# A decoder layer on one core: first loads spread over the turns, a table of context parts for each block, and three parts behind the last tile

## The chip, the core and the metric

The kernel runs on one core of one Trainium2 chip. TensorE (PE), VectorE (DVE), ScalarE (ACT), GpSimd (POOL) and SyncE (SP) run their own instruction streams and meet at semaphores. The metric is the device time in microseconds (us), from the first to the last instruction and what the launch lays around it; less is better.

## The reference, cut to what matters

One layer of a decoder: self-attention, cross-attention to a context, and a feed-forward part, each followed by a layer norm. The first half of the kernel, which the change touches, computes this:

```python
# x [8, 512, 512]: t = 8 positions, 512 columns of the batch, 512 features; 16 heads of 32
qkv = x @ in_proj_weight.T + in_proj_bias
p = (pos @ pos_proj_weight.T + pos_proj_bias).reshape(-1, h, d)
ac = jnp.einsum('tbhd,sbhd->bhts', q + r_w_bias, k)
bd = jnp.einsum('tbhd,rhd->bhtr', q + r_r_bias, p)      # then a relative shift
attn = jax.nn.softmax((ac + bd) * scale, axis=-1)
ctx = jnp.einsum('bhts,sbhd->tbhd', attn, v).reshape(t, b, e)
x = _layernorm(x + ctx @ out_proj_weight.T + out_proj_bias)
# for the second half: keys and values of the context (ctx_2048 [8, 512, 1024])
src_trans = (jnp.einsum('bsf,of->bso', src, W_src) + b_src) * src_mask[:, :, None]
```

The second half (cross-attention of 8 heads, feed-forward with rounding to an 8-bit format) reads the first half's output, the keys and the values from scratch tensors in HBM.

## The kernel before, in words

**Blocks and steps.** The first half (`phase_a`) cuts the 512 columns into NB = 4 blocks of 128 partitions. A block has 16 steps: eight score steps, in which VectorE multiplies one position's query with all keys (`score_products`) and sums over a head (`score_sums`); then the softmax; and eight value steps (`context_products`, `context_sums`), each giving one tile `ctx1` of the attention's result. Four more steps, 64 to 67, clear what is left. In the value steps TensorE makes the projections q, k and p of the next block, in the score steps v of this one. Two steps after a tile's value step comes its output projection (`output_projection`, bank `om_b`); VectorE adds the residual and takes the moments, GpSimd and ScalarE normalise, and `store_x1` stores it.

**Context parts.** Beside this run 64 parts of the context's keys and values (`QUARTERS`, the program calls them quarters too). Four parts, n%4 = 0 to 3, make a group: they read the same transposed context `cT`, made of four row blocks. Part n%4 = 0 or 1 has 50 matmuls of 256 columns, part 2 or 3 has 25 of 512. The class `FirstHalf` says how many parts a step has, in one list over the steps. In the step of part n the context rows of number n+5 are converted as well, so the last row block of a group comes with part 2 of the group before (row block 23, say, with part 18) and the group's first part can't start before it is turned.

**How a row block gets to TensorE.** SP loads it; ScalarE rounds it to float16 (`row_hi`, into one of three buffers `rows16`, which must be turned before they are used again), GpSimd makes the rest (`row_lo`), SP issues two DMA transposes (`turn`, into xT, cT or c1T). All of SP's DMAs, loads, turns and stores, go through its one in-order stream, as do those that ScalarE issues through its own. A context row is turned one step after it is converted; `exponentials` stands on ScalarE behind the row conversions of its step.

**Banks.** A part writes one of three banks `sm_b` and waits until VectorE has made `stage_lo` of part n-3; VectorE makes it one step after the part, behind that step's first product.

**The opening.** SP loads row block 0 of x, the key weights (4 x 256 KB), then x 1 to 7, and turns them as they are converted. ScalarE's queue loads the query weights (`wq_n`, 1 MB), later the position weights (`wp_n`) and the value weights (`wv_n`). TensorE transposes the weights, four transposes to a job, and alternates them with the projections k of tiles 0 to 7.

## Time and profile before

| | |
|---|---|
| median of 3 runs | 1966.91 us (1964.98 to 1968.69) |
| profiled execution | 1969.68 us, its span 1967.9 us |
| granted TensorE clock, mean | 0.981 of full speed |
| PE busy | 1849.9 us (94%) |
| DVE busy | 1336.4 us (68%) |
| ACT busy | 785.5 us (40%) |
| POOL busy | 507.2 us (26%) |
| HBM | 94.75 MB read, 33.55 MB written |

The first half ends near 847 us, when the barrier between the halves opens; the blocks' first score products start at 57.08, 252.03, 444.25 and 633.02 us. The shares above are means over both halves. TensorE's busy time counts pipelined matmuls and says nothing of how fast they run; the two levels of its clock are 1.2 and 2.4 GHz, a granted clock of 0.5 or 1.0.

### The profile page before, as it was taken

To read this page: it belongs to the slowest core of one execution; us is meant where nothing else is said; L and a number is where in the kernel's file an instruction comes from. 1 tells how busy PE (TensorE), PEld (TensorE's weight loads), DVE (VectorE), ACT (ScalarE), POOL (GpSimd) and SP (SyncE) were. 2 spreads that over 40 slices of the span, in tenths; PEclk is the share of its full clock that TensorE was granted. 3 is DMA by queue.
4 is the path that set the end of the run, shared out by engine and by line. 5 is a ranking of instruction groups with operands and counts; after the bars stand their busy time and mean duration, and the time that the engine had idled before them with its cause. 6 is when DMAs were issued, how large, how long until landed. Compare 5 with 4: busy or idle time off the path is not lost. (4 is left out here: it accounts for less than half of the span.)

```text
span 1967.9 us, 33393 instructions
## 1 busy us (share of the span) xinstructions
PE 1849.9 (94%) x12588; PEld 1016.7 (52%) x12588; DVE 1336.4 (68%) x1704; ACT 785.5 (40%) x1208; POOL 507.2 (26%) x548
## 2 busy tenths in 40 slices
PE   6998999898999999977999999999999999999988
PEld 3665455544654566545555455454454554544543
DVE  2897998799889989857565555655655556556521
ACT  3422222222222222238465364462653644626522
POOL 2134964386259326600000100001001000010010
PEclk9999999999999999979999999999999999999999
DMA  8435347525643457566312304204123041041000
GB/s 208 119 80 133 94 113 157 117 75 139 158 97 84 116 146 160 153 134 199 64 51 43 94 21 103 54 1 105 52 42 95 21 103 54 1 103 33 12 33 22
DMA packets 292139, 176.60 MB, mean 90 GB/s; under 512 B 195071, under 2 KB 248319, under 8 KB 291998
## 3 DMA queue, kind: packets, MB, share of 16 engines
q1 hardware_dynamic: 285984, 171.03, 35.6%
q10 hardware_dynamic: 6014, 3.49, 0.8%
q8 instruction: 114, 1.87, 0.4%
q14 instruction: 27, 0.22, 0.0%
HBM read 94.75 MB, written 33.55 MB: 65 GB/s over the span
## 5 line engine op out<-in xcount | busy, mean ns | idle before, releaser
L1468 DVE TENSOR_TENSOR p_lo<-k,p_hi 128x1024 f16<-128x1024 f32 x128 | 156.8, 1225 | 194.1 <-ACT p_hi L1356 194.1
L82 POOL TENSOR_TENSOR vsb<-mvb,consts 128x1 f32<-128x1 f32 x64 | 12.1, 190 | 1029.9 <-DVE mvb L1483 1029.9
L1157 PE MATMUL b_ff<-x2T_hi,w1T_hi 128*128 128x512 f16 x512 | 195.3, 381 | 2.3 <-DVE x2T_lo L1468 2.3
L1513 DVE CUSTOM_DVE_ANT_0 junk<-b_sx,mneg 128x512 f16<-128x512 f32 x256 | 176.1, 688 | 30.3 <-issue 22.3
L1157 PE MATMUL b_ff<-x2T_lo,w1T_hi 128*128 128x512 f16 x512 | 195.3, 381 | 0.0
L1157 PE MATMUL b_ff<-x2T_hi,w1T_lo 128*128 128x512 f16 x512 | 195.1, 381 | 0.0
L1388 ACT ACTIVATE k<-b_st,mbias 128x512 f32<-128x512 f32 x256 | 161.8, 685 | 14.0 <-PE b_st L1201 13.9
L574 PE MATMUL sm_b<-cT_hi,wsT_hi 128*128 128x256 f16 x512 | 142.7, 279 | 24.0 <-DMA cT_lo<-rows_lo 18.6
L775 DVE TENSOR_TENSOR prod<-q,k 128x4096 f32<-128x4096 f32 x32 | 143.1, 4472 | 20.1 <-ACT q L652 19.2
L1356 ACT ACTIVATE p_hi<-k 128x1024 f16<-128x1024 f32 x128 | 135.3, 1057 | 44.1 <-PE b_av L1216 41.7
L540 PE MATMUL pj_b<-winT_hi,xT_hi 128*128 128x512 f16 x384 | 147.3, 384 | 5.2 <-DMA xT_lo<-rows_lo 5.2
L1380 ACT ACTIVATE hq<-b_ff,b 128x512 fp8e4<-128x512 f32 x128 | 88.0, 687 | 156.6 <-PE b_ff L1157 149.9
L540 PE MATMUL pj_b<-winT_lo,xT_hi 128*128 128x512 f16 x384 | 147.2, 383 | 0.0
L540 PE MATMUL pj_b<-winT_hi,xT_lo 128*128 128x512 f16 x384 | 147.1, 383 | 0.0
L815 DVE TENSOR_TENSOR prod<-pr,v 128x4096 f32<-128x4096 f32 x32 | 142.4, 4451 | 1.1
L574 PE MATMUL sm_b<-cT_lo,wsT_hi 128*128 128x256 f16 x512 | 142.8, 279 | 0.0
L574 PE MATMUL sm_b<-cT_hi,wsT_lo 128*128 128x256 f16 x512 | 142.6, 279 | 0.0
L780 DVE TENSOR_REDUCE pr<-prod 128x128 f32<-128x4096 f32 x32 | 141.1, 4410 | 0.1
L437 POOL TENSOR_TENSOR rows_lo<-cn,rows_hi 128x512 f16<-128x512 f32 x64 | 98.5, 1546 | 79.0 <-ACT rows_hi L636 78.9
L1365 ACT ACTIVATE q<-q,rstdb 128x512 f32<-128x512 f32 x64 | 52.1, 814 | 161.7 <-POOL rstdb L88 161.7
L1157 PE MATMUL b_ff<-w2T,hq 128*128 128x512 fp8e4 x512 | 112.9, 379 | 1.6 <-ACT hq L1380 1.0
L1213 PEld LDWEIGHTS b_av<-v_hi,p_hi 128*128 128x128 f16 x1024 | 92.6, 98 | 32.1 <-DVE p_lo L1468 30.9
(270 smaller groups left out, 4318.1 us busy)
## 6 DMA issues: line engine op xcount, KB each, us to landing
cn<-in_ctx_dram SPq DMA_DIRECT2D x64, 256.0 KB, 3.3
k<-kT_scratch SPq DMA_DIRECT2D x24, 512.0 KB, 8.0
x<-in_x_dram SPq DMA_DIRECT2D x32, 256.0 KB, 3.0
x_scratch<-x SPq DMA_DIRECT2D x32, 256.0 KB, 2.2
q<-x_scratch SPq DMA_DIRECT2D x8, 1024.0 KB, 5.6
q<-x_scratch SPq DMA_DIRECT2D x32, 256.0 KB, 4.0
out_dram<-q SPq DMA_DIRECT2D x32, 256.0 KB, 3.8
xn<-in_x_dram SPq DMA_DIRECT2D x24, 256.0 KB, 2.9
```

The lines of the kernel that those rows point to most:

```text
L437: pool.tensor_tensor(lo[:, :], row_source(kind, i), hi[:, :], ALU.subtract).then_inc(s["row_lo"], 1)
L540: pe.matmul(out, a, c, start=(j == 0 and m == 0), stop=False)
L574: pe.matmul(dst, a, z, start=(j == 0 and m == 0), stop=False)
L775: dve.tensor_tensor(prod[:, :, :], q[:, t, :].unsqueeze(1).to_broadcast([P, T, E]), k[:, :, :], ALU.mult).then_inc(s["sc_prod"], 1)
L780: dve.tensor_reduce(pr[:, t].rearrange("p h s -> p s h"), prod[:, :, :].rearrange("p s (h d) -> p s h d", h=H1), AX.X, ALU.add).then_inc(s ...
L815: dve.tensor_tensor(by_head(prod), probs, by_head(v), ALU.mult).then_inc(s["av_prod"], 1)
L1157: mm = pe.matmul(out, a, c, start=(start and n == 0), stop=end)
L1213: pe.matmul(dst, hi[:, st, rows], v_hi[:, st, h, :], start=(st == 0), stop=False)
L1356: act.activation(dst, src, ACT.Copy, scale=scale).then_inc(done, 1)
L1388: act.activation(pf[:, st, :], st_b[st % 2][:, :], ACT.Exp, bias=mbias[:, st:st + 1], scale=D2 ** -0.5).then_inc(s["st_exp"], 1)
L1468: dve.tensor_tensor(dst, bank, hi, ALU.subtract).then_inc(out, 1)
L1513: dve.tensor_tensor_reduce(junk[:, :], sx_b[tt % 2][:, :], mneg[:, :], 1.0, NEG, ALU.add, ALU.max, mx[:, h % 2, tt:tt + 1]).then_inc(s["sx ...
```

## The change

It does four things. (1) SP loads x 3 to 7 one at a time, each behind the turn of the row block three before it; the loads `load_ring` and the first context rows move behind turns 5 to 7. On ScalarE's queue the query weights go behind the conversion of the key weights, in four DMAs instead of one, the position weights two projections later and the value weights three later. (2) The row of positions has a semaphore of its own, so its transposes don't wait for the three columns of biases. (3) The counts of context parts differ by block. In the table below a stroke joins parts of one step; it is worked out from the two lists:

```
            score steps (8)                         value steps (8)
block 1  b  8/9 10 11 12/13 14 15 16/17 18          19/20 21 22 - - - - -
         a  8/9 10 11 12/13 14 15 16/17 18          19 20/21 22 - - - - -
block 2  b  23/24 25 26 27/28 29 30 31/32 33        34/35 36 37 - - - - -
         a  23 24/25 26 27 28/29 30 31 32/33        34 35 36/37 - - - - -
block 3  b  38/39 40 41 42/43 44 45 46/47 48        49/50 51/52 53/54 55/56 57/58 59/60 61/62 63
         a  38 39 40/41 42 43 44/45 46 47           48/49 50/51 52/53 54/55 56/57 58 59 60
after    b  -
         a  61/62 63
```

(4) In steps 64 and 65 TensorE makes the parts 61, 62 and 63, each step's parts ahead of its output projection.

```diff
-    SCORES_FIRST = (0, 0, 0, 0, 1, 1, 1, 1)
-    SCORES = (2, 1, 1, 2, 1, 1, 2, 1)
-    VALUES = (2, 1, 1, 0, 0, 0, 0, 0)
-    VALUES_LAST = (2, 2, 2, 2, 2, 2, 2, 1)
+    SCORES = ((0, 0, 0, 0, 1, 1, 1, 1), (2, 1, 1, 2, 1, 1, 2, 1), (1, 2, 1, 1, 2, 1, 1, 2), (1, 1, 2, 1, 1, 2, 1, 1))
+    VALUES = ((2, 1, 1, 0, 0, 0, 0, 0), (1, 2, 1, 0, 0, 0, 0, 0), (1, 1, 2, 0, 0, 0, 0, 0), (2, 2, 2, 2, 2, 1, 1, 1))
+    TAIL = (2, 1, 0, 0)
...
-            for t in range(1, T):
-                sp.dma_start(k[:, t, :], x_in[0, t]).then_inc(x_first[t], 16)
+            for t in range(1, 3):
+                load_first_x(t)
             for kind, i in plan.first_uses:
                 if kind == "x" or i < 4:
                     turn(kind, i)
+                if kind == "x" and i + 3 < T:
+                    load_first_x(i + 3)
                 if (kind, i) == ("x", 1):
                     load_mask(0)
-                if kind == "x" and 2 <= i < 5:
-                    load_ring(i - 2)
+                if kind == "x" and 5 <= i:
+                    load_ring(i - 5)
...
-                pe.wait_ge(s["small_ld"], 16 * 4)
+                pe.wait_ge(s["pos_ld"], 16)
...
             for g in range(8, plan.STEPS):
+                tail = g >= 16 * NB
+                if tail:
+                    for n in plan.quarters(g):
+                        context_products(n)
                 for n in plan.tiles(g - 2):
                     output_projection(n)
-                for n in plan.quarters(g):
-                    context_products(n)
+                if not tail:
+                    for n in plan.quarters(g):
+                        context_products(n)
...
-            act.dma_start(wq_n, d.in_w[0:E, :].rearrange("(o p) k -> p o k", p=P)).then_inc(win_ld["wq"], 16)
             for n in range(WK, WQ):
                 weights_hi(n)
                 if n % 2:
                     row_hi(*firsts[(n + 1) // 2])
+            for o in range(4):
+                act.dma_start(wq_n[:, o, :], d.in_w[o * P:(o + 1) * P, :]).then_inc(win_ld["wq"], 16)
...
-                if t == 0:
+                if t == 2:
                     for o in range(4):
                         act.dma_start(wp_n[o], d.pos_w[o * P:(o + 1) * P, :]).then_inc(win_ld["wp"], 16)
-                if t == 2:
+                if t == 5:
                     act.dma_start(wv_n, d.in_w[2 * E:3 * E, :].rearrange("(o p) k -> p o k", p=P)).then_inc(
```

SP's stream at its start, before (`k` is the buffer of x, `prod` that of the key weights, `rows_0` to `rows_2` the converted rows):

```order
L374 DMA k<-in_x_dram 128x512
L376 DMA prod<-in_in_w_dram 128x512 x4
L378 DMA k<-in_x_dram 128x512 x7
L330 DMA_TRANSPOSE xT_hi<-rows_0_hi 128x4x128 [waits A_row_lo]
L330 DMA_TRANSPOSE xT_lo<-rows_0_lo 128x4x128
L330 DMA_TRANSPOSE xT_hi<-rows_1_hi 128x4x128 [waits A_row_lo]
L330 DMA_TRANSPOSE xT_lo<-rows_1_lo 128x4x128
```

and of the change:

```order
L373 DMA k<-in_x_dram 128x512
L377 DMA prod<-in_in_w_dram 128x512 x4
L373 DMA k<-in_x_dram 128x512 x2
L328 DMA_TRANSPOSE xT_hi<-rows_0_hi 128x4x128 [waits A_row_lo]
L328 DMA_TRANSPOSE xT_lo<-rows_0_lo 128x4x128
L373 DMA k<-in_x_dram 128x512
L328 DMA_TRANSPOSE xT_hi<-rows_1_hi 128x4x128 [waits A_row_lo]
L328 DMA_TRANSPOSE xT_lo<-rows_1_lo 128x4x128
```

Five of the seven loads have left the place ahead of the first turn. ScalarE's stream at the start of block 1's value steps, before (`pr<-pr` is the exponential):

```order
L636 ACTIVATE rows_1_hi<-xn 128x512 [waits A_xn_ld1,A_turned1]
L636 ACTIVATE rows_2_hi<-cn 128x512 [waits A_cn_ld0,A_turned2]
L636 ACTIVATE rows_0_hi<-cn 128x512 [waits A_cn_ld1,A_turned0]
L672 ACTIVATE pr<-pr 128x1024 [waits A_probs]
L662 ACTIVATE stage_hi<-sm_b,small 128x512 [waits A_mk_scaled,A_st_out1,A_sm_filled]
L662 ACTIVATE stage_hi<-sm_b 128x512 [waits A_st_out0,A_sm_filled]
```

and of the change:

```order
L644 ACTIVATE rows_1_hi<-xn 128x512 [waits A_xn_ld1,A_turned1]
L644 ACTIVATE rows_2_hi<-cn 128x512 [waits A_cn_ld0,A_turned2]
L680 ACTIVATE pr<-pr 128x1024 [waits A_probs]
L670 ACTIVATE stage_hi<-sm_b,small 128x512 [waits A_mk_scaled,A_st_out1,A_sm_filled]
L660 ACTIVATE q<-pj_b 128x512 [waits A_pj_filled,A_sc_done]
```

One context row and its wait for a turned buffer no longer stand ahead of the exponential; in blocks 0 and 3 that row stays. VectorE's end of the first half, before, from the last tile's last sum (`ctx<-prod`) on:

```order
L826 TENSOR_TENSOR ctx<-prod 128x512 [waits A_av_half,A_row_lo]
L764 SCALAR_TENSOR_TENSOR stage_lo<-sm_b,small,stage_hi 128x512 [waits A_sm_hi]
L832 SCALAR_TENSOR_TENSOR x_0<-om_b,x_0 128x512 [waits A_res_ld0,A_om_filled]
L835 BN_STATS small<-x_0 128x6 [waits A_om_used]
L837 BN_AGGR small<-small 128x2 [waits A_ln_stats]
L832 SCALAR_TENSOR_TENSOR x_1<-om_b,x_1 128x512 [waits A_res_ld1,A_om_filled]
```

and of the change:

```order
L835 TENSOR_TENSOR ctx<-prod 128x512 [waits A_av_half,A_row_lo]
L773 SCALAR_TENSOR_TENSOR stage_lo<-sm_b,stage_hi 128x512 [waits A_sm_hi]
L841 SCALAR_TENSOR_TENSOR x_0<-om_b,x_0 128x512 [waits A_res_ld0,A_om_filled]
L844 BN_STATS small<-x_0 128x6 [waits A_om_used]
L846 BN_AGGR small<-small 128x2 [waits A_ln_stats]
L773 SCALAR_TENSOR_TENSOR stage_lo<-sm_b,stage_hi 128x512 [waits A_sm_hi]
L773 SCALAR_TENSOR_TENSOR stage_lo<-sm_b,small,stage_hi 128x512 [waits A_sm_hi]
L841 SCALAR_TENSOR_TENSOR x_1<-om_b,x_1 128x512 [waits A_res_ld1,A_om_filled]
```

Four `stage_lo` instead of one come after the last tile: three of them behind it here, and one more, of part 63, after the last rows shown.

## Rows read from the trace of the kernel before

**Rows 1.** Windows: length; busy PE, PEld, DVE, ACT, POOL; granted clock; DMA share; GB/s
```profile
444.00:633.00 189.00, 180.18 (x1097) 104.36 (x1096) 169.06 (x94) 50.41 (x87) 110.95 (x67) 0.98 0.49 119
633.00:847.00 214.00, 198.06 (x1181) 117.69 (x1179) 184.45 (x110) 47.44 (x76) 103.28 (x77) 0.96 0.56 140
```

**Rows 2.** Waits of TensorE, 0 to 57 us: total, times, longest
```profile
PE om_b L487 <- DMA bcols<-in_rr_dram: 5.5, 1, 5.5
PE pj_b L540 <- DMA xT_lo<-rows_lo: 5.2, 2, 3.0
```

**Rows 3.** Source and tile views, opening: wq load, first transposes, wp loads
```profile
L723 ACTq DMA_DIRECT2D v<-in_in_w_dram x1: 742/742/742, 5.7 to 5.7; - x1
...
DMA to landing us min/median/max: 14.7/14.7/14.7
...
L330 SPq DMA_TRANSPOSE xT_hi<-rows_hi x8: 1200/1319/3103, 7.6 to 41.5; - x8
...
DMA to landing us min/median/max: 2.6/5.3/12.5
...
L737 ACTq DMA_DIRECT2D cT_hi<-in_pos_w_dram x2: 352/401/450, 26.8 to 27.2; - x2
...
DMA to landing us min/median/max: 2.9/3.5/4.1
```

**Rows 4.** Timeline, opening: start, duration, engine, what, [idle before <- releaser]
```profile
11.51 1.39 DVE L842 SCALAR_TENSOR_TENSOR winT_lo<-sm_b,winT_hi 128x512 f16<-128x512 f32 x2 [0.31 <-ACT winT_hi L677]
...
20.67 0.59 PE L540 MATMUL pj_b<-winT_hi,xT_hi 128*128 128x512 f16 x1 [3.00 <-DMA xT_lo<-rows_lo]
...
25.74 0.61 PE L543 MATMUL pj_b<-rows,pick 128*128 128x512 f16 x1
...
29.22 0.38 PE L543 MATMUL pj_b<-rows,pick 128*128 128x512 f16 x1
...
32.46 0.38 PE L543 MATMUL pj_b<-rows,pick 128*128 128x512 f16 x1
```

**Rows 5.** Timeline of block 1, around its exponential and a later residual
```profile
354.13 0.63 ACT L636 ACTIVATE rows_hi<-cn 128x512 f16<-128x512 f32 x1 [2.07 <-DMA cT_lo<-rows_lo]
...
354.25 0.37 PE L574 MATMUL sm_b<-cT_hi,wsT_hi 128*128 128x256 f16 x1 [5.67 <-DMA cT_lo<-rows_lo]
...
355.74 1.22 DVE L801 TENSOR_REDUCE ctx<-pr 128x128 f32<-128x1024 f32 x1 [8.58 <-ACT pr L672]
...
397.35 0.69 DVE L832 SCALAR_TENSOR_TENSOR x<-om_b,x 128x512 f32<-128x512 f32 x1 [2.55 <-PE om_b L555]
```

**Rows 6.** Waits of block 2, 444 to 633 us
```profile
PE sm_b L574 <- DMA cT_lo<-rows_lo: 6.5, 1, 6.5
DVE ctx L801 <- ACT pr L672: 5.6, 1, 5.6
...
DVE x L832 <- PE om_b L555: 2.8, 1, 2.8
```

**Rows 7.** Waits of block 3, 633 to 847 us
```profile
DVE x L832 <- PE om_b L555: 13.0, 6, 8.1
...
PE om_b L554 <- DMA c1T_lo<-rows_lo: 4.2, 1, 4.2
...
PE sm_b L574 <- DVE stage_lo L764: 3.9, 1, 3.9
...
PE sm_b L574 <- DMA cT_lo<-rows_lo: 3.2, 2, 2.9
```

**Rows 8.** Timeline, last matmul of output projections (L555) and of a part
```profile
823.98 0.38 PE L555 MATMUL om_b<-rows,pick 128*128 128x512 f16 x1
...
829.38 0.38 PE L583 MATMUL sm_b<-rows,pick 128*128 128x512 f16 x1
...
832.18 0.38 PE L555 MATMUL om_b<-rows,pick 128*128 128x512 f16 x1
...
841.88 0.44 PE L555 MATMUL om_b<-rows,pick 128*128 128x512 f16 x1
```

More of the change, by code:

```diff
@@ L136, in __init__ @@
         for b in range(NB):
-            counts += self.SCORES if b else self.SCORES_FIRST
-            counts += self.VALUES if b < NB - 1 else self.VALUES_LAST
+            counts += self.SCORES[b] + self.VALUES[b]
+        counts += self.TAIL
         at, self.by_step = 0, []
@@ L154, in quarters @@
     def quarters(self, g):
-        return self.by_step[g] if 0 <= g < 16 * NB else []
+        return self.by_step[g] if 0 <= g < self.STEPS else []
     def tiles(self, g):
@@ L239, in phase_a @@
     pos_b, gb = om_b[1], om_b
-    names = ("made", "zeroed", "step", "small_ld", "bias_ld", "wt_filled", "wt_hi", "wt_lo", "pos_filled", "pos_ready",
+    names = ("made", "zeroed", "step", "small_ld", "pos_ld", "bias_ld", "wt_filled", "wt_hi", "wt_lo", "pos_filled", "pos_ready",
              "pb_ready", "g0_filled", "g_filled", "g_hi", "g_lo", "row_hi", "row_lo", "pj_filled", "pj_copied", "sm_filled", "sm_hi", "sm_lo", "om_filled", "om_used",
@@ L388, in _ @@
                 if kind == "c" and i + 2 < 5:
-                    load_rows(kind, i + 2)
+                    load_rows("c", i + 2)
             for use in plan.loads_after(-1):
@@ L470, in weight_transposes @@
                     if n % 4 == 0:
-                        pe.wait_ge(win_ld[("wk", "wq", "wp", "wv")[n // 4]], 64 if n in (WK, WP) else 16)
+                        pe.wait_ge(win_ld[("wk", "wq", "wp", "wv")[n // 4]], 16 if n == WV else 64)
                 else:
@@ L867, in bias_columns @@
             def bias_columns():
-                dve.wait_ge(s["small_ld"], 16 * 4)
+                dve.wait_ge(s["small_ld"], 16 * 3)
                 for z in range(2):
```

6 lines of the change are left out of this document (4 added, 2 removed).

## The prediction, made before the changed kernel ran

> **What bounds the kernel now.** I read the windows first, with their edges at the blocks' first score products. In block 2 TensorE is busy for 180.2 of 189 us and VectorE for 169.1; in block 3 it is 198.1 and 184.5 of 214 [rows 1]. Neither engine has much room, and what is lost is lost where one waits for the other or for a transpose. So the second view is the waits, block by block, and only the last, the timeline around the longest of them, says what each one waited for.
>
> The unit of TensorE's work comes from rows 8: an output projection ends 2.80 us after the part before it, a part 5.40 us after the projection before it (829.38 - 823.98). A projection q, k or v has the same 13 matmuls, so 2.8 us too; with a weight's four transposes it is 3.24 us (32.46 - 29.22) [rows 4]. The first one after a long wait takes longer: its last matmul starts 5.1 us after its first (25.74 - 20.67) [rows 4], where 12 of 13 matmuls at full clock take 2.6. I take 1.5 us as the price of the lower clock behind each wait of some 3 us or more; the granted clock of 0.96 to 0.98 in both windows [rows 1] says that such stretches exist.
>
> **The opening: -9.2 us.** TensorE waits 3.0 us for the first turned row block and 2.2 us for the sixth (5.2 in two) [rows 2]. The first pair of transposes is issued from 7.6 us on and takes up to 12.5 us to land, against 2.6 at its best; the query weights, 1 MB on the other queue, take 14.7 us [rows 3]. Ahead of the turn SP has put seven loads of x, 1.8 MB. The change leaves two of them there and holds the query weights back, so the turn is issued at about 6.6 us and lands near 12 even at twice the best landing. The key weights are complete on VectorE at 12.9 [rows 4], and that becomes the start of the first projection; the wait of 5.5 us for a bias column, which has kept TensorE from anything else until 17 [rows 2], is gone with its own semaphore. At the lower clock the projection then ends at about 18.4 instead of 26.4: -8.0. The sixth row block's wait goes with its lower clock: -3.7.
>
> What comes late instead: the query weights are issued when ScalarE is free, 12.9 to 14.7, and land 4.1 us after the last issue if they behave as the position weights' loads did [rows 3]: 18.8 against a need at 18.4. The position weights are issued behind the third projection, until about 27.7, and land at 31.8 against a need at 31. Each turned row block must pass load, 0.6 us of ScalarE, 1.2 us of GpSimd, 2.5 us of issue and 2.6 us of landing, 11.0 us with a load of 4.1, for three buffers: 3.7 us for each against TensorE's 3.24, over five blocks 2 us. I put 2.5 us for the three together, so -9.2. Bounds: with nothing late -11.7; with the query weights at their old 14.7 us (27.6 instead of 18.4) nearly all is lost, about -2. The value weights come 10 us ahead of their need and wait only if they too take 14.7 us: 4.7 us at worst. What the opening gains stays, since VectorE's first product waits for the first query's copy and both engines are dense behind it.
>
> **Block 1: -4.5 us.** Part 20 waited 5.67 us for its group's last row block while VectorE waited 8.58 us for the exponential, which stood behind a conversion that itself waited 2.07 us for a buffer [rows 5]. The table moves part 20 and that conversion one step on. ScalarE reaches the exponential 2.7 us earlier (2.07 + 0.63). TensorE runs q, k and p of the next block (6.5 us) in place of its wait. VectorE's later wait of 2.55 us for the output projection of tile 9 [rows 5] shrinks, because that projection comes 5.67 us, and the 1.5 us of lower clock, earlier; but tile 8's projection now runs into its own turn and gives about 2.5 back. I count 2.6 + 1.9 = 4.5; bounds 2.0 and 5.2.
>
> **Block 2: -6 us.** Part 28 waits 6.5 us [rows 6], and here the new table has separated 27 from 28 as well as 23 from 24 and 31 from 32. The score steps hold 8 v, 11 parts and 2 output projections: 22.4 + 59.4 + 5.6 = 87.4 us of TensorE. With row block 31 turned one part earlier nothing is waited for, and the softmax comes 6.5 + 1.3 us earlier, the exponential, with one conversion less ahead, 2 us more. That is 10. But parts 36 and 37 are now in one step, ahead of tile 17's output projection: VectorE waits there for 10.8 us of parts instead of 5.4, about 7 us instead of 2.8 [rows 6]. Net -6; bounds -2 (the wait moves to another turn) and -8.
>
> **Block 3 and the tail: -11 us.** TensorE's work is 8 v, 26 parts and 10 output projections: 22.4 + 140.4 + 28 = 190.8 us. It starts 0.9 us before the block's first product and could end 190 us after it; it ends at 209.3 (842.3 - 633.0) [rows 8], behind 11.3 us of waits (3.2 + 3.9 + 4.2) [rows 7] and the lower clock after them. Of these the 3.2 goes as in block 2. The last 4.2, for the turn of the last tile, is covered by parts 61 to 63 (16.2 us), and with it the lower clock. The 3.9 stays and gets worse: part 51 now needs `stage_lo` of part 48, which VectorE makes only after the softmax and one more product (before, part 52 met this with 49), and then part 52 needs row block 55, which is converted behind tile 24's rows. Step by step I get waits of 3.8 and about 3 us there, and an end at 198 us: -11. Bounds: -5 (both last waits double) and -16 (only 2 us lost in all). VectorE's wait for the last projection, 8.1 of its 13.0 us [rows 7], turns into waiting for the parts and costs nothing.
>
> The second half gets the same work. Sum: -9.2 - 4.5 - 6 - 11 = -30.7. A walk from wait to wait misses small new ones, so I keep -29. From the profiled execution (1969.7) that is 1940.7; it lies 2.8 us above the median of the runs shown, so the forecast for the median is 1938. A measurement of this kernel tells about 0.2% (4 us) from no change.
>
> **A rule weighed.** The late loads are covered in rows: three turns take 9.7 us of TensorE, a 256 KB load lands in 2.9 to 4.1 us [rows 3]. The Trainium skill (DMA: Bandwidth & Descriptors, Rules for kernel authors) says the opposite of the change: issue a DMA early and wait late, so that its fixed cost overlaps. By it the five late x loads would sit on the path; no row shows that they must, and the loads that were early are those that held the first transposes.
>
> **The rivals.**
> - *Only the ends pay.* In the middle blocks VectorE needs 169 of 189 us [rows 1], so TensorE's waits are partly its own slack, and each removed wait could reappear in front of the next output projection, as I have it once in block 2. Then the opening (-9.2) and the tail (-4.2 - 1.5) are all: -15, 1952. For it: VectorE's 13.0 us of such waits. Against: the exponential's waits of 8.6 and 5.6 us [rows 5, 6] are waits of both engines at once. Chance 0.19.
> - *The turn loop.* If transposes go on landing in 12.5 us, because wq, wp and the late x loads still share the DMA engines, the loop of three buffers takes 20.9 us, 7.0 for each row block against 3.24: five blocks cost 19 us and eat the start's 8 and more. The opening is +10, all together -11: 1956. The rule above would have it on this side. Against: the transposes' median of 5.3 us holds while such loads already run beside them [rows 3]. Chance 0.09.
> - *Slower.* With two parts in a value step TensorE and VectorE could take turns instead of overlapping: the part needs `stage_lo` from behind the product, VectorE then needs the output projection behind both parts. At block 2's 7 us in each of the seven such steps of blocks 1 to 3 it costs 49 us, less the 29: +20, 1987. It decides above 4.2 us a step. Against: seven steps of two parts stand in block 3 already, and outside the last wait VectorE lost 4.9 us in five of them [rows 7]. Chance 0.04.
> - *Nothing*, gains and losses within 4 us: 0.02.
>
> The forecast as worked out, between -20 and -40, has the rest, 0.66. The range 1926 to 1954 holds it nearly whole and most of the first rival; below it lie the bounds of all places at once, above it the turn loop and the slower case. Faster 0.94, same 0.02, slower 0.04.
>
> **What the changed profile would show.** The first k projection at about 13 us instead of 20.7, and VectorE's first product near 48 instead of 57. No wait for cT of 5 us or more in the steps of parts 20, 28 and 40. The exponential's waits on VectorE down to about 6, 2 and 1 us in blocks 1 to 3; a wait of about 7 us for an output projection in block 2; a wait of about 4 us for `stage_lo` at part 51 and none for the last tile's turn. Blocks 1 and 2 of 187.7 and 183 us between their first products, instead of 192.2 and 188.8. Wrong would make it: transposes that still land in 10 us, SP so full that a group's last row is late in the new place too, or a wait at part 51 that VectorE passes on to each later step.

## The result, and the profile after

The changed kernel takes 1969.93 us (median of 20 runs), the kernel of before 1965.78 us beside it: a ratio of 1.0018, 95% interval 1.0011 to 1.0025. It is slower by 0.2%, some 4 us, where 29 us less were forecast. The profiled execution has a span of 1967.8 us, against 1967.9: that of before lay 3.9 us above its median, that of the changed kernel at it, so the two traces show less of the loss than the medians do. Below, a lead is how much earlier than in before an event comes, and a hold is something that keeps a row's transposes from being issued.

The windows of the changed kernel, with their edges at its own first score products of blocks 2 and 3 (columns as in [rows 1]):

```profile
440.00:633.00 193.00, 182.72 (x1095) 104.86 (x1094) 170.57 (x93) 49.90 (x87) 121.55 (x66) 0.97 0.48 116
633.00:848.00 215.00, 197.20 (x1181) 116.91 (x1179) 181.71 (x110) 47.50 (x76) 96.56 (x78) 0.97 0.55 139
```

Block 2 is 4 us longer than in [rows 1], with the same instructions but for one or two; GpSimd is busy 11 us longer (121.55 against 110.95). The waits say what filled it. First TensorE's in the opening (the query weights, then the position weights), which answer to [rows 2]:

```profile
PE sm_b L484 <- DMA v<-in_in_w_dram: 2.2, 1, 2.2
PE sm_b L484 <- DMA cT_lo<-in_pos_w_dram: 1.6, 1, 1.6
```

Then block 1 (249 to 440 us) and block 2 (440 to 633), which answers to [rows 6]:

```profile
PE om_b L557 <- DMA c1T_lo<-rows_lo: 6.6, 4, 4.3
PE sm_b L577 <- DMA cT_lo<-rows_lo: 2.5, 1, 2.5
...
PE om_b L557 <- DMA c1T_lo<-rows_lo: 6.5, 4, 4.3
PE sm_b L577 <- DMA cT_lo<-rows_lo: 3.8, 2, 2.1
...
DVE x L841 <- PE om_b L558: 7.6, 1, 7.6
...
DVE ctx L810 <- ACT pr L680: 5.5, 1, 5.5
```

And block 3 (633 to 848), against [rows 7]:

```profile
PE om_b L557 <- DMA c1T_lo<-rows_lo: 5.7, 1, 5.7
PE sm_b L577 <- DMA cT_lo<-rows_lo: 4.0, 2, 3.0
PE sm_b L585 <- DVE stage_lo L773: 3.9, 1, 3.9
...
DVE x L841 <- PE om_b L558: 23.2, 6, 10.0
```

The 6.5 us at part 28 are gone, but a wait of 4.3 us stands at an output projection in block 1 (tile 8, which waited for nothing in before; the longest such wait of block 1, 2.5 us, was tile 6's) and again in block 2 (tile 16, where before had none longer than 1 us), and in block 3 one of 5.7 at tile 28 took the place of the 4.2 at tile 31. The waits on context rows became waits on tiles.

The table follows that through the first half. The start of the second score product (us from the start of the span) stands for the opening; "block 1" and "block 2" run from one block's first product to the next one's, "block 3" from its first product to the end of the last output projection ("last o"). All are read from the timelines, one profiled execution each; the ratio comes from the timed runs of that kernel and of before on the same chip. Medians of before in the six comparisons lie between 1965.8 and 1970.1 us, and a profiled execution lies up to 3.9 us from its kernel's median. The changed kernel itself was timed only in the first comparison, so its ratio stands beside the others across comparisons; ratios are compared best where they were measured together: runs 1 to 4, 5 to 8, 9 to 12, 13 to 16, and 17 and 18. The part behind the last projection, which no run changes, takes 1121.8 to 1128.8 us by the traces. The block lengths are steadier, but not exact: block 2 with the new table took 193.2 to 193.6 us in four kernels (after, runs 3, 4 and 17), block 1 with the same code 183.3 to 186.1 in another four (runs 10, 12, 14 and 15).

| kernel | ratio (95% interval) | 2nd product | block 1 | block 2 | block 3 | last o |
|---|---|---|---|---|---|---|
| before | 1 | 70.3 | 192.2 | 188.8 | 209.3 | 842.3 |
| after | 1.0018 (1.0011 to 1.0025) | 67.8 | 191.0 | 193.4 | 210.7 | 843.8 |
| 1 loads only | 0.9992 (0.9979 to 1.0006) | 66.9 | 192.0 | 188.7 | 209.3 | 839.8 |
| 2 old block 2 | 0.9985 (0.9973 to 0.9997) | 66.0 | 190.3 | 194.2 | 212.6 | 843.0 |
| 3 old block 3 | 0.9994 (0.998 to 1.0008) | 63.8 | 191.0 | 193.6 | 208.9 | 840.3 |
| 4 old block 1 | 1.0014 (1.0001 to 1.0027) | 64.1 | 191.9 | 193.2 | 210.5 | 840.5 |
| 5 after, four buffers | 1.0005 (0.9995 to 1.0015) | 67.9 | 191.6 | 192.7 | 210.8 | 843.8 |
| 6 before, four buffers | 0.9985 (0.9973 to 0.9996) | 68.1 | 193.4 | 188.8 | 209.3 | 838.6 |
| 7 parts ahead of o16 | 0.9985 (0.9976 to 0.9995) | 66.6 | 190.6 | 188.8 | 208.8 | 835.8 |
| 8 low rows on VectorE | 1.0023 (1.0013 to 1.0033) | 65.2 | 190.7 | 196.7 | 211.1 | 844.5 |
| 9 parts ahead, three tiles | 0.9985 (0.9973 to 0.9996) | 65.3 | 190.2 | 189.4 | 209.9 | 836.7 |
| 10 turns ahead of stores | 0.9964 (0.9952 to 0.9976) | 66.0 | 186.1 | 189.9 | 209.7 | 835.0 |
| 11 both holds removed | 0.9958 (0.9944 to 0.9973) | 67.3 | 185.0 | 183.2 | 213.1 | 832.0 |
| 12 run 9 + run 10 | 0.9944 (0.9931 to 0.9957) | 69.5 | 183.3 | 185.3 | 213.9 | 836.1 |
| 13 before, turns ahead | 0.9999 (0.9983 to 1.0015) | 69.6 | 187.2 | 188.2 | 208.1 | 836.9 |
| 14 run 10, old block 3 | 0.9965 (0.9951 to 0.9979) | 67.2 | 184.0 | 190.2 | 206.8 | 834.0 |
| 15 run 10, stage_lo ahead | 0.9978 (0.9964 to 0.9992) | 67.3 | 184.1 | 188.8 | 212.8 | 837.5 |
| 16 together | 0.9947 (0.9928 to 0.9966) | 62.7 | 185.5 | 184.9 | 209.3 | 826.4 |
| 17 context loads ahead | 1.0001 (0.9988 to 1.0013) | 65.4 | 190.8 | 193.6 | 210.7 | 841.2 |
| 18 together, one part behind | 0.9898 (0.9883 to 0.9914) | 64.8 | 186.7 | 183.2 | 202.9 | 820.8 |

### The profile page after: what moved, and what is told of

Read it like the earlier page. It is cut to its first block and busy times, and to the rows that moved or that the text cites. A ratio compares the mean times of both kernels' runs of the same rounds, so it can differ in the third digit from the quotient of the medians.

```text
span 1967.8 us, 33396 instructions
## 1 busy us (share of the span) xinstructions
PE 1849.1 (94%) x12588; PEld 1014.7 (52%) x12588; DVE 1337.2 (68%) x1704; ACT 783.9 (40%) x1208; POOL 516.1 (26%) x548
## 5 line engine op out<-in xcount | busy, mean ns | idle before, releaser
L1477 DVE TENSOR_TENSOR p_lo<-k,p_hi 128x1024 f16<-128x1024 f32 x128 | 156.9, 1225 | 193.6 <-ACT p_hi L1365 193.6
L577 PE MATMUL sm_b<-cT_hi,wsT_hi 128*128 128x256 f16 x512 | 141.1, 276 | 12.9 <-DMA cT_lo<-rows_lo 11.3
L440 POOL TENSOR_TENSOR rows_lo<-cn,rows_hi 128x512 f16<-128x512 f32 x64 | 113.6, 1781 | 67.5 <-ACT rows_hi L644 67.4
L1222 PEld LDWEIGHTS b_av<-v_hi,p_hi 128*128 128x128 f16 x1024 | 92.6, 98 | 31.9 <-DVE p_lo L1477 30.7
```

The lines of the kernel that those rows point to most:

```text
L440: pool.tensor_tensor(lo[:, :], row_source(kind, i), hi[:, :], ALU.subtract).then_inc(s["row_lo"], 1)
L577: pe.matmul(dst, a, z, start=(j == 0 and m == 0), stop=False)
L1222: pe.matmul(dst, hi[:, st, rows], v_hi[:, st, h, :], start=(st == 0), stop=False)
L1477: dve.tensor_tensor(dst, bank, hi, ALU.subtract).then_inc(out, 1)
```

## Where block 2's lead goes: tile 16

Softmax and exponential of block 2 come 6.0 us earlier than before (first value product at 541.88 against 547.84). Tile 20's value product starts at 592.1 in the changed kernel and at 592.0 in before: all is gone within four tiles. The timelines of SyncE, GpSimd, VectorE and TensorE show how (start, duration, engine, what, [idle before]), with one more row of GpSimd's, for tile 28:

```profile
555.83 0.36 SPq L348 DMA_DIRECT2D v_scratch<-stage_hi  x1
556.24 0.43 SPq L348 DMA_DIRECT2D v_scratch<-stage_lo  x1
556.78 1.19 SPq L328 DMA_TRANSPOSE c1T_hi<-rows_hi  x1
558.01 1.26 SPq L328 DMA_TRANSPOSE c1T_lo<-rows_lo  x1
...
551.49 4.67 POOL L440 TENSOR_TENSOR rows_lo<-ctx,rows_hi 128x512 f16<-128x512 f32 x1 [5.10 <-ACT rows_hi L644]
...
549.99 0.69 DVE L835 TENSOR_TENSOR ctx<-prod 128x512 f32<-128x512 f32 x1
550.72 4.42 DVE L824 TENSOR_TENSOR prod<-pr,v 128x4096 f32<-128x4096 f32 x1
555.06 0.74 DVE L773 SCALAR_TENSOR_TENSOR stage_lo<-sm_b,small,stage_hi 128x512 f16<-128x512 f32 x1
...
791.02 1.16 POOL L440 TENSOR_TENSOR rows_lo<-ctx,rows_hi 128x512 f16<-128x512 f32 x1 [4.15 <-ACT rows_hi L644]
...
560.58 0.61 PE L557 MATMUL om_b<-woT_hi,c1T_hi 128*128 128x512 f16 x1 [4.26 <-DMA c1T_lo<-rows_lo]
```

Tile 16's context row is done at 550.68. Its turn is issued 6.1 us later, and two things end just before: GpSimd's subtraction, which begins while VectorE's product runs and lasts 4.67 us (without one beside it 1.16: tile 28's, at 791.02), and the store of a finished part, which stands ahead of the turn in SyncE's queue and waits for a `stage_lo` that VectorE makes behind its product. TensorE stands for 4.26 us, and the projection behind that wait takes 5.31 us instead of 2.97. Then come parts 36 and 37 with q, k and p, and VectorE waits 7.6 us for tile 17's projection. The waits of SyncE from 440 to 560 us give the size of the second hold:

```profile
SPq L348 <- DVE stage_lo L773: 9.6, 2, 9.0
```

## The experiments

**Runs 1 to 4: the change in pieces.** Run 1 is the changed kernel with the tables of before; the others put one part of them back:

```
 run 2, block 2: SCORES[2] = (2, 1, 1, 2, 1, 1, 2, 1), VALUES[2] = (2, 1, 1, 0, ...)
 run 3, block 3: SCORES[3] = (2, 1, 1, 2, 1, 1, 2, 1), VALUES[3] = (2, 2, 2, 2, 2, 2, 2, 1), TAIL = (0, 0, 0, 0)
 run 4, block 1: VALUES[1] = (2, 1, 1, 0, ...)
```

> The first loads of the change with the tables of before. Theory (what a tile's turn takes sets each block; a lead is given back at the next turn only where parts stand ahead of it differently): block 1's first product comes 3.3 us earlier, as in the changed kernel, and since the tables are those of before the lead is kept to the end: about 3 us faster than before (0.9985). Rival (block steps are held by something that does not move with the opening, or the loads are what costs): no faster than before, or slower.

> The changed kernel with block 2's two rows of the table as in before (parts 27/28 in one step, value steps of 2, 1, 1 parts). Theory: block 2 gives back what it gained at tile 16's output projection because parts 36 and 37 stand behind it; with the old rows block 2 takes 189 us instead of 193.4 and the whole is 3 to 5 us faster than the changed kernel (about 1966). Rival (the lead would be lost anyway): the same as the changed kernel, 1970.

> The changed kernel with block 3 as in before and no tail. Theory: the tail saves the last turn's wait (4.2 us and 1.5 us of lower clock) but block 3's late turns of tiles 24 and 28 (PE waits of 3.0 and 5.7 us) cost as much; with the old rows the block takes 209 to 210 us and the whole is within 3 us of the changed kernel, 1967 to 1972. Rival (the tail itself is a gain and only the earlier blocks lose): 5 to 8 us slower than the changed kernel, 1975 or more.

> The changed kernel with block 1's value steps as in before (2, 1, 1). Theory: block 1 then takes 192 us instead of 191.0, and block 2 gives everything back at tile 16 in both, so the time is that of the changed kernel within 1.5 us (1970). Rival (block 1's gain of 1.2 us survives to the end, as a sum over blocks has it): 1 to 3 us slower than the changed kernel.

Run 1: with the old tables the opening's lead stays to the end (block 1 starts at 249.7 instead of 252.0, the last projection ends 2.5 us early); its ratio leaves anything from 4 us faster to 1 us slower. Run 3: block 3 takes 208.9 us in its old form and 210.7 in the new one, where 11 us less were forecast. Run 4: block 1's new value row is worth 0.9 us. Run 2 missed in part: its ratio is 6.5 us better than that of the changed kernel, but block 2 did not fall to 189 us in its trace, and its last projection ends only 0.7 us earlier. Block 2 took 194.2 us: a lead of 7.9 us ran into the rows of parts 28 (3.4 us) and 32 (2.2), and VectorE waited 8.8 us for the exponential, which stood on ScalarE behind the conversion of an x row whose load was waited for (4.13 us, at 536.08). Then TensorE waits at tile 16 here too, though three parts stand ahead of it as in before:

```profile
564.11 0.39 PE L557 MATMUL om_b<-woT_hi,c1T_hi 128*128 128x512 f16 x1 [4.12 <-DMA c1T_lo<-rows_lo]
```

So the old row is no cure by itself. What counts at tile 16 is how far TensorE is ahead of VectorE, whose sum the row needs, and the number of parts is only one way to change that.

**Runs 5 and 6: four pairs of row buffers.** `RING = 4` in the changed kernel and in before (raw_g lies in ctx1 to make room).

> The changed kernel with four pairs of row buffers ahead of the turns instead of three (a row may be converted while three others wait for or are in their turn). Theory A (the chain of turns itself, conversion, turn, landing, buffer free again, has hardly less to do in a block than TensorE, so a lead of TensorE runs into it and is lost there): the leads are kept, no wait for a context row block in block 2 (3.4 us at part 28 in the last run with the old rows), and the whole is 5 to 12 us faster than before, 1956 to 1963. Theory B (only the late turn of the block's first tiles, held by GpSimd's conversion under VectorE's product, takes the lead back): nearly the time of the changed kernel, 1967 to 1971.

> The kernel of before with four pairs of row buffers. Theory A: the waits for cT in block 1 (5.67 us) and block 2 (6.5 us) shrink by more than half, 5 to 15 us faster than before. Theory B: these waits stand (the row is late by its load, conversion and turn, not by its buffer), within 2 us of before.

Theory A falls. Block 2 is 192.7 us in run 5 and still loses its lead at tile 16 (wait of 3.6 us); in run 6 the waits for cT of 5.7 and 6.5 us stand as they were and blocks 1 to 3 are as long as before or longer. Its 3 us in the ratio are 1 more than theory B allowed; in its trace they come from ahead of block 1, whose first product starts at 247.0 us instead of 252.0. The buffers do not hold the rows.

**Run 7: the order inside one step.** In the step of tile 16's projection (42) the two parts go ahead of it:

```diff
-                tail = g >= 16 * NB
+                tail = g >= 16 * NB or g == 42
```

> The changed kernel with parts 36 and 37 ahead of tile 16's output projection in the one step where they stand behind it. Theory (TensorE waited 4.3 us for tile 16's turn there and VectorE then 7.6 us for tile 17's projection, because two parts lay between them): the wait for the turn is covered by the parts, VectorE's wait falls to about 3 us, block 2 takes 4 us less, and block 3 starts 4 us earlier; of that 1 to 4 us are left at the end (1966 to 1969). Rival (the lead is lost at the next turn anyway): block 3 starts at the same time as in the changed kernel and the whole is 1970.

As the theory has it: in block 2 TensorE's longest wait for a tile is 1.2 us, VectorE's for a projection 2.4 instead of 7.6, block 2 takes 188.8 us instead of 193.4, block 3 starts 6 us earlier (1.5 of them from before block 2), and the ratio falls from 1.0018 to 0.9985, 6.5 us, where 1 to 4 were expected.

**Run 8: GpSimd's hold alone.** For tiles 8, 16 and 28 VectorE makes the low half behind the sum, and GpSimd skips it:

```diff
                     context_sums(b, t)
+                    if 8 * b + t in (8, 16, 28):
+                        row_lo_here(8 * b + t)
+            def row_lo_here(i):   # u is the row's number, hi and lo its buffers
+                dve.wait_ge(s["row_hi"], u + 1)
+                dve.wait_ge(s["row_lo"], u)
+                dve.tensor_tensor(lo[:, :], row_source("o", i), hi[:, :], ALU.subtract).then_inc(s["row_lo"], 1)
```

> The changed kernel with the low half of three tiles' context row (tiles 8, 16 and 28, the late ones) made by VectorE right behind the sum instead of by GpSimd, where it took 4.67 us for tile 16 while VectorE's next product ran, against 1.16 us alone. VectorE loses about 1.8 us for each (wait for the high half and the subtraction), 5.4 us in all. Theory (GpSimd's lock makes these turns late): TensorE's waits of 4.3, 4.3 and 5.7 us shrink by 3 to 4 us each; the whole is 0 to 5 us faster than the changed kernel. Rival (these turns are late by SyncE's queue and their buffer): the waits stay, 3 to 5 us slower.

The rival's mechanism came true, the waits stay, though its price did not: the ratio is 1 us above the changed kernel's, not 3 to 5. The rows tell why the waits stay. VectorE and SyncE in this kernel:

```profile
550.32 0.69 DVE L785 TENSOR_TENSOR rows_lo<-ctx,rows_hi 128x512 f16<-128x512 f32 x1 [0.76 <-ACT rows_hi L648]
550.93 4.42 DVE L835 TENSOR_TENSOR prod<-pr,v 128x4096 f32<-128x4096 f32 x1
...
556.03 0.36 SPq L349 DMA_DIRECT2D v_scratch<-stage_hi  x1
556.44 0.43 SPq L349 DMA_DIRECT2D v_scratch<-stage_lo  x1
556.98 1.19 SPq L329 DMA_TRANSPOSE c1T_hi<-rows_hi  x1
```

The row is complete at 551.0 instead of 556.2, and the turn is issued at the same time, behind the store. TensorE's wait for tile 16 even grew, to 6.7 us, and block 2 takes 196.7 us. For tile 28 the edit cost far more than the 1.8 us expected. VectorE's idle time before these three rows:

```profile
  ACT rows_hi L648: 10.7, 3
```

Two of the three are 0.76 us, which leaves 9.2 for tile 28: its high half, ScalarE's, comes that late.

**Run 9: parts ahead for tiles 28 and 29 too** (`g == 42 or g >= 62`).

> The changed kernel with the parts ahead of the output projection in the step of tile 16 (as in the last run) and in the steps of tiles 28 and 29 too (part 59 ahead of tile 28's projection, 60 ahead of tile 29's). Theory (a wait for a tile's turn costs only where no part is ready to run under it): the wait of 5.7 us for tile 28's turn and 2.3 us of lower clock behind it fall away; the last output projection ends 6 to 8 us earlier than with tile 16 alone (835.8), near 829, and the whole is 1957 to 1960. Rival (VectorE, which then waits longer for tile 28's projection, sets the end): within 2 us of the kernel with tile 16 alone, 1963 to 1966.

The rival's time (0.9985, as in run 7), but not its reason. Tile 28's wait is 0.8 us, and part 60, now reached sooner, waits for its context row instead:

```profile
795.62 0.39 PE L557 MATMUL om_b<-woT_hi,c1T_hi 128*128 128x512 f16 x1 [0.81 <-DMA c1T_lo<-rows_lo]
803.88 0.37 PE L577 MATMUL sm_b<-cT_hi,wsT_hi 128*128 128x256 f16 x1 [5.28 <-DMA cT_lo<-rows_lo]
```

**Runs 10 to 12: the queue.** Inside a step SyncE's turns of x rows and of the tile's row go ahead of the stores (run 10); this and VectorE's low rows (run 11); this and the parts ahead (run 12):

```diff
-                for n in plan.quarters(g - 1):
-                    store_stage(n)
                 for use in plan.turns(g):
                     if use[0] != "c":
                         turn(*use)
+                for n in plan.quarters(g - 1):
+                    store_stage(n)
```

> The changed kernel with SyncE's queue in another order inside a step: the turns of x rows and of the tile's context row ahead of the stores of finished parts, which wait for stage_lo. For tile 16 both GpSimd's conversion (done at 556.2 us) and the store's wait (stage_lo done at 555.8) end together, so by this theory removing one alone moves nothing there: tile 16's wait stays near 4 us; for tile 28 the turn was issued 7 us after its row was ready, behind two turns and four stores, and comes 2.3 us earlier: 0 to 4 us faster than the changed kernel. Rival (the stores behind hold their buffers longer and ScalarE waits for them): slower than the changed kernel.

> The last run's order of the queue and, for tiles 8, 16 and 28, the low half of the row made by VectorE (as in the run before). Theory (two holds end together at tile 16: GpSimd's conversion under VectorE's product and the store's wait for stage_lo, so each alone moved nothing): now the turn of tile 16 is issued near 551 us instead of 556.8, TensorE's wait of 4.3 to 6.7 us for it is gone, and the same for tile 8; the lead at block 3's start is 3 to 6 us where it was 0. VectorE pays 1.8 us for each of three tiles. Rival (a third hold, landing or buffer): the wait stays above 3 us.

> The parts ahead of the output projection for tiles 16, 28 and 29, and the turns ahead of the stores. If the two are independent, as the theory has it, their gains add for tiles that are still waited for (8 and 12 to 14, some 0.5 to 1 us each, and part 56's row): 1 to 4 us faster than the parts alone. Rival: no difference to the parts alone, or slower since the stores come late.

Run 10 gives more than was expected (0.9964, against 1.0018 some 10 us where 0 to 4 were expected), and where it was not looked for: block 1 goes from 191.0 to 186.1 us (tile 8's wait of 4.3 us is gone, and the softmax is earlier). Part of this is taken from block 0, which the table leaves out: from the second product to block 1's first it takes 183.2 to 185.8 us in the eight kernels with this queue and 179.0 to 183.1 in the twelve others. In run 10 TensorE waits 2.1 us there for the row of part 4, at the lower clock behind it, instead of 1.0. So the queue's gain in block 1 is to be taken with some 3 us less. Tile 16 still waits 4.2 us, for GpSimd; block 2 is 3.5 us shorter all the same, because the wait of 2.1 us at part 32 and 1.7 us of lower clock behind it are gone. Run 11 takes both holds away; its waits of block 2, TensorE's and VectorE's:

```profile
PE om_b L561 <- DMA c1T_lo<-rows_lo: 2.3, 3, 0.9
PE sm_b L581 <- DMA cT_lo<-rows_lo: 2.2, 1, 2.2
...
DVE x L852 <- PE om_b L562: 0.8, 1, 0.8
```

Block 2 is 183.2 us, the figure that the forecast's "blocks 1 and 2 of 187.7 and 183 us" had asked for. Two holds that end together show nothing at tile 16 when one is removed (run 8; run 10) and 6.7 us of the block when both are (189.9 to 183.2; over all runs, 188.8 to 190.2 with the queue alone and 183.2 to 184.9 with both, runs 11, 16 and 18). But block 3 grew to 213.1 us, and of the 24 us by which run 11's last softmax is ahead of that of before 10 are left at the last projection; the median is that of run 10 beside it (1960.3 against 1960.9 us). One reason is the edit itself, at tile 28:

```profile
777.28 0.69 DVE L785 TENSOR_TENSOR rows_lo<-ctx,rows_hi 128x512 f16<-128x512 f32 x1 [10.90 <-ACT rows_hi L648]
```

ScalarE makes that high half behind the conversions of parts 56 and 57, which wait for TensorE, and all of VectorE stands for it. In run 12, without that edit but with the parts ahead, block 3 is 213.9 us, and part 60 waits 6.4 us for its row as in run 9. By the medians run 12 is 7 us faster than run 9 beside it (1958.3 against 1965.5), where 1 to 4 were expected; its profiled execution was 3 us slower than its median, and that of run 9 3 us faster, so the traces hide this.

**Runs 13 to 16: what is the tables' and what the queue's.** Run 13 is before with run 10's queue, run 14 is run 10 with the old block 3, run 15 is run 10 with `stage_lo` of parts 48 and 49 ahead of the product in the step of part 51, run 16 puts together runs 10 and 15, the low rows of tiles 8 and 16 and run 17's edit.

> The kernel of before with the turns ahead of the stores in SyncE's queue, nothing else. Theory (the queue held the turns only where the change had put a part into the step ahead of tile 16's turn and the like; the new tables are worth something once it is freed): 0 to 4 us faster than before, and so 4 to 10 us slower than the changed kernel with the same order (0.9964). Rival (the order of the queue is the whole gain and the tables are worth nothing): 0.996 to 0.997, as the changed kernel with that order.

> The changed kernel with the turns ahead of the stores and block 3 as in before, no tail. The forecast put 11 us on block 3 and the tail. Theory (the new rows only move the waits to tiles 28 and 29 and part 56, as in the traces so far): within 3 us of the changed kernel with the same order of the queue, 0.995 to 0.998. Rival (with the queue freed the forecast's term holds): 6 us or more slower than that, 0.999 or more.

> The changed kernel with the turns ahead of the stores, and in the one step of part 51 VectorE makes stage_lo of parts 48 and 49 ahead of its product instead of behind it. Theory (block 3 is bound by TensorE from its softmax on, so each wait of it counts in full): the wait of 3.9 us at part 51, and 1.7 us of lower clock, go; part 52's wait for a stage_lo (1.7) goes too; the last projection ends 4 to 6 us earlier. Rival (TensorE then waits for tile 24's or 28's turn by as much): 0 to 2 us.

> The turns ahead of the stores, low rows of tiles 8 and 16 on VectorE, stage_lo ahead of the product in part 51's step, and in the opening each context row's load ahead of the turn of the row two before it. Theory: the opening's first value products come 2 us earlier still (VectorE's wait of 2.8 us and TensorE's of 3.6 us behind the conversion that waits for the third context row go down), the rest adds up to a last projection near 826 us; 0.991 to 0.994. Rival (each frees time that the next turn takes): as the best so far, 0.9944 to 0.996.

Run 13 measures no gain for the queue alone in before (0.9999), run 10 with the change has 0.9964: by the ratios the change is worth 7 us once the queue is freed. Run 14, which has its opening and its tables of blocks 1 and 2, stands beside run 13: 1962.0 against 1967.6 us, 5.6 us. The traces give it less: run 13's last projection ends at 836.9, run 10's at 835.0 and run 14's at 834.0, and block 2 is no shorter (188.2 against 189.9 and 190.2). Of the difference between 5.6 us and these 2.9, 1.6 are that run 13's profiled execution was 3.1 us below its median and run 14's 1.5, and 1.1 stand behind the last projection, where the code is the same. So the size of this stays open between 2 and 7 us. Run 14 is clear: block 3 and the tail in their new form are worth nothing with the queue freed either (0.9965 against 0.9964; 206.8 us against 209.7). Run 15 shows one reason. TensorE's waits of its block 3:

```profile
PE sm_b L578 <- DMA cT_lo<-rows_lo: 9.5, 2, 6.5
PE om_b L558 <- DMA c1T_lo<-rows_lo: 5.0, 2, 3.6
```

The 3.9 us for `stage_lo` are gone, and part 52 waits 6.5 us for its row instead of 1.7 for a `stage_lo`. The last projection ends 2.5 us later than in run 10, where 4 to 6 us earlier were expected. In block 3 TensorE is ahead of the rows, whichever wait is removed. Run 16 has the earliest last projection so far (826.4), but its ratio is that of run 12: the 0.991 to 0.994 expected were not reached.

**Run 17: the opening's context loads**, each ahead of the turn that it stood behind:

```diff
             for kind, i in plan.first_uses:
+                if kind == "c" and i + 2 < 5:
+                    load_rows("c", i + 2)
                 if kind == "x" or i < 4:
                     turn(kind, i)
```

> The changed kernel with each context row's load in the opening ahead of the turn of the row two before it. Theory: ScalarE's two waits of 5.7 us for these loads shrink to about 1 us, VectorE's wait of 2.8 us behind its first sum goes, and the second score product starts 2 to 5 us earlier (62.7 instead of 67.8, as with all together); since the queue's other order is unchanged the lead is then lost at tile 16, and the whole is within 2 us of the changed kernel. Rival (the opening's lead is kept to the end): 2 to 4 us faster than the changed kernel, 1966 or less.

ScalarE's timeline in the changed kernel, and behind it the same conversions in run 17:

```profile
49.46 0.63 ACT L644 ACTIVATE rows_hi<-cn 128x512 f16<-128x512 f32 x1 [5.66 <-DMA cn<-in_ctx_dram]
...
57.71 0.63 ACT L644 ACTIVATE rows_hi<-cn 128x512 f16<-128x512 f32 x1 [5.64 <-DMA cn<-in_ctx_dram]
```

```profile
49.93 0.63 ACT L644 ACTIVATE rows_hi<-cn 128x512 f16<-128x512 f32 x1 [3.89 <-DMA cn<-in_ctx_dram]
...
54.63 0.63 ACT L644 ACTIVATE rows_hi<-cn 128x512 f16<-128x512 f32 x1 [2.08 <-DMA cn<-in_ctx_dram]
```

The waits shrink from 11.3 to 6.0 us, where about 1 us was expected, and the last conversion comes 3.1 us earlier. The second product starts at 65.4; in the three kernels with this edit it starts at 64.3 on average (runs 16 to 18), in the 14 executions of the change's opening without it at 66.5. So it is worth some 2 us, less than one execution scatters. In this one trace what is won stays to the end (last projection 2.6 us earlier; 1.0001 instead of 1.0018), as the rival had it and against the theory, which had it lost at tile 16: block 2 costs its 4.6 us once (193.6 us here), and a lead from outside passes through it.

**Run 18: the last block as before, with one part behind the last tile.** Run 16 without its `stage_lo` edit, and

```
 VALUES[3] = (2, 2, 2, 2, 2, 2, 1, 1), TAIL = (0, 1, 0, 0), SCORES[3] as in before
```

> Turns ahead of stores, low rows of tiles 8 and 16 on VectorE, context loads ahead of turns in the opening, tables of the change in blocks 1 and 2, and block 3 as in before but with its last part behind the last tile, ahead of the last output projection. Theory: block 3 takes 206.8 us from its first product to the last projection with the old rows and this order of the queue; the wait of 4.35 us for the last tile's turn and 1.7 us of lower clock are covered by the one part: 201 us, so the last projection ends near 818 to 820 us and the whole is 1945 to 1950 (0.989 to 0.992). Rival (the one part only moves to where VectorE or another turn waits): block 3 of 206 us or more and 0.993 to 0.995.

0.9898, 1949.97 us: faster than both kernels, by some 20 us, and as expected (its last projection ends at 820.8, the expectation's 818 to 820 and 201 us for block 3 were a little low). Block 3 takes 202.9 us, 3.9 less than run 14: of the 4.35 us and the lower clock behind it, part 63 covers all, but tile 30's turn shows with 1.7. Its windows of blocks 2 and 3:

```profile
434.00:618.00 184.00, 179.54 (x1100) 104.02 (x1099) 170.45 (x96) 49.89 (x88) 110.64 (x68) 1.00 0.51 123
618.00:821.00 203.00, 192.76 (x1181) 115.65 (x1178) 180.90 (x107) 46.66 (x75) 103.73 (x73) 0.99 0.58 146
```

TensorE is busy for 97.6% of block 2, at a granted clock of 1.00. That leaves some 4 us for another order of steps to win there.

## Why the prediction was wrong, by its own steps

- **The opening, -9.2.** The first projection starts at 13.10 us, as forecast (13), and its last matmul is 8.5 us early (17.24 against 25.74; forecast 8.0). Two terms failed behind that. One is the price of the late weights: TensorE waits 2.2 us for the query weights and runs at the lower clock behind that, so the second projection's last matmul is only 5.0 us early (24.24 against 29.22), and 1.6 us for the position weights: some 5 us in all, where 2.5 were set aside for these and the row blocks together. With the sixth row block's wait gone the lead is 7.2 us at the seventh projection (39.71 against 46.89). The other is the context rows' loads: the last transposes ahead of the first product wait for ScalarE, which stood for a context row's load until 49.46:

```profile
51.12 0.66 PE L484 MATMUL sm_b<-ident,v 128*128 128x128 f32 x4 [1.08 <-ACT q L685]
```

The first score product starts at 51.65 against 57.08: -5.4, not -9.2. Then 2.9 us more are given back before the second. "Five blocks, 3.7 us each" named each row block's path, but not the context rows' loads, which stand in SyncE's queue behind the turns; run 17 shows that moving them gives some of it back. The 14 executions of the change's opening start the second product between 63.8 and 69.5 us, the three of the old one at 68.1, 69.6 and 70.3: the term was worth some 3 us. The three edits of the opening (x loads, weights, semaphore of the positions) were never run apart, so what each is worth is not shown.
- **Block 1, -4.5.** The mechanism was right (the exponential's wait 8.6 to 6.2, the first value product some 3 us earlier in its block), the account behind it not: tile 8's turn was to take about 2.5 us back. It takes 4.3 us of waiting and 2.4 of lower clock (the projection takes 5.42 us against 2.97), where before had neither; that term is the step that was mis-sized. -1.2 measured.
- **Block 2, -6.** This step failed, with 4.6 us on the other side. "With row block 31 turned one part earlier nothing is waited for" was nearly so (parts 28 and 32 wait 1.7 and 2.1 us). VectorE's 7 us for tile 17 came as forecast (7.6). The step that failed is the path of TensorE to tile 16, which the sum put at nothing. With two parts ahead of tile 16's projection instead of three it gets there before the turn, which neither GpSimd nor SyncE's queue lets go before VectorE's product is over: a wait of 4.3 us and 2.3 of lower clock. Run 7 removes the wait by order, run 11 by its two causes; both give block 2 its time back. Run 2 waits there behind three parts too, so what counts is TensorE's lead over VectorE, not the number of parts as such.
- **Block 3 and the tail, -11.** The softmax is 10 us early, the last turn's 4.2 us are covered, part 51 waits 3.9: all as written. The sum counted only "about 3 us" of waits behind part 51 and left out the rest of TensorE's path. In its place came 1.0 us at part 52, 3.0 us and 1.7 of lower clock at part 56's row, and tile 28's turn (5.7 us and 2.3 of lower clock), where ScalarE's conversion stood behind part 57's and SyncE had two turns and four stores ahead of it: row complete at 792.2, turn issued at 799.2. +1.4 measured. Runs 14 and 15 each took one thing back, the rows of the table and the wait at part 51, and neither gained by it; putting the old rows back with one part behind the last tile did (run 18).
- **The rivals.** "Only the ends pay" had the mechanism, a removed wait that comes back ahead of the next output projection, and stopped short: it comes back at the ends too. "The turn loop" did not come: the eight transposes of x rows into `xT_hi` landed in 2.7 to 7.3 us, the first in 3.8 where it had been 12.5. The rule weighed there speaks on this side in part: the Trainium skill (DMA: Bandwidth & Descriptors, Rules for kernel authors) would issue a DMA early and wait late, and the loads that came to stand late, those of the context rows, cost the opening some 2 us (run 17). For the x loads nothing in the trace speaks for it: TensorE's first projection is 7.6 us earlier without five of them ahead of the turns. But the query weights left the other queue at the same time, and no run separates the two. The slower case was a mechanism at 49 us in seven steps; only one of them cost anything like its price.

By the traces the sum is: block 1 starts 3.4 us early, block 1 gives 1.2 more, block 2 takes 4.6 back and block 3 1.4, so the last projection ends 1.5 us later than before (843.8 against 842.3), where 30.7 us earlier had been added up.

What stays open: the worth of the tables with the queue freed (2 to 7 us), what each edit of the opening gives, and why block 0 grows with the queue's new order beyond the wait at part 4. Tile 28's hold on ScalarE is read from rows; no run removed it.

## What to carry to other kernels

When an order is changed to take a wait away from one engine, follow the engine to its next input from elsewhere and ask whether that input can come earlier as well; if its path goes through an engine or a queue that does not come earlier too, the lead is lost there. In a queue that works in order, put what somebody waits for ahead of what only has to be stored: here the store waited up to 9 us for its data with the turn behind it. And a hold that does nothing when removed may have a twin that ends at the same time; remove both before it is dismissed.

## What the runs showed of the hardware

GpSimd's subtraction of a 128x512 row took 1.16 us alone. Each of the six times in the changed kernel's trace that one of a tile's row began 0.8 us into a 4.42 us product of VectorE, it took 4.67 and ended 1.0 us behind the product, which is nearly its own length; moved to VectorE it took 0.69. It is not the company alone that slows it: beside a VectorE reduction of 4.41 us, which reads one tile, two of them took 2.27 us together:

```profile
456.71 2.27 POOL L440 TENSOR_TENSOR rows_lo<-cn,rows_hi 128x512 f16<-128x512 f32 x2
...
455.01 4.41 DVE L789 TENSOR_REDUCE pr<-prod 128x128 f32<-128x4096 f32 x1
```

The Trainium skill (SBUF — State Buffer, Who interferes with whom) has this as an exclusive lock of the port that both engines share, held by VectorE's instruction with two SBUF inputs; these rows agree with it. A projection of 13 matmuls behind a wait of 4.26 us took 5.31 us instead of 2.97, 0.43 from one matmul to the next instead of 0.22, at a granted clock of 0.50 (560.6 to 565.2 us): 1.2 in place of 2.4 GHz. Part 32, behind a wait of 2.1 us, took 7.29 instead of 5.62, at 0.50 from 517.6 to 520.9. So waits shorter than the 3 us from which the prediction counted the lower clock can bring it too, though not each time (part 28, behind 1.7 us: 5.62), and its price was 1.7 to 2.4 us in these places, not 1.5. The opening differs between executions of the same code by up to 5.7 us at the second product, and in four kernels that are nearly alike behind it the order is kept to the last output projection (64.1, 65.4, 67.8 and 67.9 us there; 840.5, 841.2, 843.8 and 843.8 at its end: runs 4 and 17, the changed kernel, run 5).
